# Row stacks by selection matmuls and resident experts in a gated cross-attention and mixture block

## What is computed

```
x  = x + tanh(g0) * attention(layernorm(x), ctx, Wq, Wk, Wv)      # one head of 128, 512 keys per sequence
X  = layernorm(x);  h = rmsnorm(X)
q, k, v = h @ wq, h @ wk, h @ wv                                   # 16 heads of 8
X  = X + softmax(q k^T / sqrt(8)) v @ wo                           # 256 x 256 per head and sequence
h2 = rmsnorm(X);  probs = softmax(h2 @ router)                     # 8 experts, top 2
moe = swiglu(h2, shared) + sum_e combine[:, e] * swiglu(h2, expert e)   # width 256, all 8 experts on all tokens
x  = x + tanh(g1) * (X + moe)
```

## Time and profile before

| | |
|---|---|
| median of 3 runs | 249.63 us |
| the profiled execution's own time | 249.14 us |
| its span, first to last instruction | 247.4 us |
| PE busy | 202.7 us (82%) |
| DVE busy | 152.5 us (62%) |
| ACT busy | 101.3 us (41%) |
| POOL busy | 58.8 us (24%) |
| mean granted TensorE clock | 0.922 |

### The profile page before, as it was taken

The page is one execution under the profiler, slowest core; times in us unless marked ns, Lnnn a source line. Parts: engine busy times, 40 slices in busy tenths (PEclk is TensorE's granted clock), DMA queues, the critical chain, the costliest instruction groups (busy, mean ns, idle before and its releaser), DMA issues.

```text
span 247.4 us, 3838 instructions
## 1 busy us (share of the span) xinstructions
PE 202.7 (82%) x1327; PEld 161.2 (65%) x1327; DVE 152.5 (62%) x393; ACT 101.3 (41%) x203; POOL 58.8 (24%) x77
## 2 busy tenths in 40 slices
PE   7699695659783798299888577899789999999994
PEld 5467464446572566167665455688668888888883
DVE  3779999647653175446687642478874654655653
ACT  8153265930162274246584565423231221221320
POOL 8566969310140020011011011003302332000000
PEclk9999998865679599869999999999979999999999
DMA  6900002535934023400000010000002230000002
GB/s 175 269 0 4 0 16 72 153 104 121 229 103 105 7 90 85 91 3 5 9 1 5 3 48 0 3 0 0 4 0 64 87 107 0 21 3 1 1 3 85
DMA packets 7124, 12.83 MB, mean 52 GB/s; under 512 B 992, under 2 KB 4576, under 8 KB 6592
## 3 DMA queue, kind: packets, MB, share of 16 engines
q1 hardware_dynamic: 7104, 12.58, 19.1%
HBM read 9.69 MB, written 2.62 MB: 50 GB/s over the span
## 4 chain that ended last, share of the span: by engine, by line
PE 48%; DVE 19%; DMA 12%; SPq 11%; issue 3%; ACT 3%; POOL 2%; DVEq 0%; ACTq 0%; POOLq 0%
PE bank L1066 12%; PE bank L1083 7%; PE bank L1085 6%; PE bank L1084 6%; DMA split_scratch<-split 5%; DMA q_st<-negmT 5%; PE bank L1052 5%; SPq L320 4%; SPq L323 4%; PE bank L1037 4%; PE bank L1026 3%; DVE mxs L822 2%; DVE xs L696 1%; DVE small L703 1%; DVE y L690 1%
## 5 line engine op out<-in xcount | busy, mean ns | idle before, releaser
L822 DVE TENSOR_REDUCE mxs<-bank 128x2 f32<-128x512 f32 x64 | 42.5, 689 | 27.9 <-PE bank L1026 27.4
L588 ACT ACTIVATE ep<-bank 128x512 f32<-128x512 f32 x64 | 37.5, 595 | 35.3 <-PE bank L1037 34.7
L1037 PE MATMUL bank<-q_st,k_st 128*128 128x256 f32 x128 | 28.8, 311 | 16.7 <-DMA q_st<-negmT 13.3
L1026 PE MATMUL bank<-k_st,q_st 128*128 128x256 f32 x128 | 34.3, 363 | 2.2 <-DVE mxs L822 1.1
L1066 PEld LDWEIGHTS bank<-down_s,vx 128*128 128x128 f32 x288 | 34.9, 193 | 1.8 <-issue 0.4
L1066 PE MATMUL bank<-down_s,vx 128*128 128x128 f32 x288 | 35.2, 276 | 0.0
L612 ACT ACTIVATE silu<-bank 128x512 f32<-128x512 f32 x28 | 16.6, 598 | 43.9 <-PE bank L1085 43.9
L1037 PEld LDWEIGHTS bank<-q_st,k_st 128*128 128x128 f32 x128 | 21.9, 210 | 18.5 <-DMA q_st<-negmT 13.9
L1083 PE MATMUL bank<-h2hi,whi 128*128 128x512 f32 x72 | 30.8, 428 | 2.7 <-ACT silu L612 2.7
L1026 PEld LDWEIGHTS bank<-k_st,q_st 128*128 128x128 f32 x128 | 23.5, 231 | 10.5 <-issue 4.5
L1085 PE MATMUL bank<-h2hi,wlo 128*128 128x512 f32 x72 | 29.1, 404 | 0.0
(11 more groups left out here) (139 smaller groups left out, 288.4 us busy)
## 6 DMA issues: line engine op xcount, KB each, us to landing
raw<-expert_w SPq DMA_DIRECT2D x9, 256.0 KB, 3.7
split_scratch<-split SPq DMA_DIRECT2D x16, 128.0 KB, 2.2
q_st<-split_scratch SPq DMA_DIRECT2D x16, 128.0 KB
k_st<-split_scratch SPq DMA_DIRECT2D x16, 128.0 KB
down_s<-expert_w SPq DMA_DIRECT2D x9, 128.0 KB, 2.7
ctxT<-ctx_T SPq DMA_DIRECT2D x1, 672.0 KB, 7.7
xs<-x_tiles SPq DMA_DIRECT2D x2, 256.0 KB, 4.2
out_dram<-x SPq DMA_DIRECT2D x2, 256.0 KB, 2.0
```

The costliest lines, as they stand in the source:

```text
L588: nc.scalar.activation(ep[:, n % NEP].rearrange("p t s -> p (t s)"), b_of(("exp", n))[:], ACT.Exp, scale=SCALE_H).then_inc(free(("exp", n) ...
L822: nc.vector.tensor_reduce(mxs[:, n // NH, :, n % NH], b_of(("max", n))[:].rearrange("p (t s) -> p t s", t=TB), AX_X, ALU.max).then_inc(fre ...
L1026: last = pe.matmul(b_of(("max", n))[:, j * L:(j + 1) * L], q_st[:, b % NSTACK, h // 2, j * P:(j + 1) * P], k_st[:, b % NSTACK, k_slot(h), ...
L1037: last = pe.matmul(b_of(("exp", n))[:, j * L:(j + 1) * L], k_st[:, b % NSTACK, k_slot(h), j * P:(j + 1) * P], q_st[:, b % NSTACK, h // 2, ...
```

## The change

Five things change together.

1. **Stacks by matmul.** The DRAM scratch, `stack` and its 12 DMAs per sequence go. Two matrices of zeros and ones (`sel_q` of 96 columns, `sel_k` of 64, per pair of heads; built by POOL from the identity) pick the rows: stage `e` i (four per sequence, 16 in all) does 8 matmuls of 256 columns into two "proj" banks. DVE (sequence 0) or ACT (sequences 1 to 3) copies the q stack, 512 columns, and ACT copies the k stack in two pieces of 512 columns and 32 partitions. There are two stacks instead of three. ACT fills the picking rows twice instead of three times.
2. **Maxima without a DMA.** DVE writes the maxima into columns 64 on of a zeroed tile; the PE transposes 96 columns, and ACT writes the negated rows straight into `q_st`, broadcast to four places (1024 columns), so `place_m` goes.
3. **The order by hand.** The x slots become single steps (`f g xn q s p o n h k w e`) in `FIRST_STEPS`, ahead of the first a slot, and `MIXED_STEPS`, after certain a slots. `LAG` is 12 instead of 13, and the steps after a sequence's last head come one slot earlier.
4. **Experts resident and per sequence.** All nine experts' split weights stay in SBUF. An item is one expert on one sequence: 12 matmuls of 256 columns and half as many down-products; there are 36. Loads no longer wait for places.
5. **Items late.** An item follows every a slot from 76 on. The last exponential of the attention is in slot 63 + 12 = 75, so no item stands ahead of it, `tanh_items` is empty and every item uses Silu. The routing of sequences 2 and 3 falls on slots 90 (first exponential), 92 and 93. The output is stored per sequence.

The core of the diff:

```
-NSTACK = 3
-LAG = 13
+LAG = 12
+NSTACK = 2
-C_STEPS = [("uT0", 31, 31), ("uT1", 32, 32), ("cT", 34, 34), ("wo", 36, 36), ("square", 37, 37), ("h2", 38, 38),
-           ("h2T", 41, 41), ("router", 43, 43)]
-ROUTE_STEPS = [("route_exp1", 43, 43), ("route_top", 45, 45), ("route_exp2", 45, 45), ("route_weights", 46, 46)]
+M_STEPS = [("mT0", 8, 8), ("mT1", 16, 16)]
+C_STEPS = [("uT0", 30, 30), ("uT1", 31, 31), ("cT", 33, 33), ("wo", 35, 35), ("square", 36, 36), ("h2", 37, 37),
+           ("h2T", 40, 40), ("router", 42, 42)]
+ROUTE_STEPS = [("route_exp1", 42, 42), ("route_top", 44, 44), ("route_exp2", 44, 44), ("route_weights", 45, 45)]
+FIRST_STEPS = """f0 g0 xn0 f1 q0 g1 s0 xn1 s1 p0 q1 o0 p1 s2 o1 f2 s3 n0 p2 g2 h0 o2 xn2 p3 k0
+                 e0 q2 e1 o3 e2 w0 e3 n1""".split()
+MIXED_STEPS = {0: "s4 h1", 1: "f3", 2: "k1 s5", 3: "p4 g3", 4: "e4 xn3", 5: "o4 p5", 6: "e5 q3", 7: "o5 s6", 8: "e6 n2",
+               9: "p6 s7", 10: "e7 h2", 11: "o6", 12: "p7 k2", 13: "w1", 14: "o7", 16: "n3", 17: "e8", 19: "h3",
+               21: "e9 k3", 25: "e10", 29: "e11", 31: "w2", 33: "e12", 37: "e13", 41: "e14", 45: "e15", 47: "w3"}
+EARLY_FROM, EARLY_EVERY = 76, 1
...
+            def make_stacks(i):
+                b, part = i // 4, i % 4
...
+                for qk, use, rows in ((0, ("stq", i), sel_q), (1, ("stk", i), sel_k)):
+                    may_fill(pe, use)
+                    for n in range(2):
+                        for hl in range(2):
+                            last = pe.matmul(b_of(use)[0:NSEL if qk == 0 else 64, n * L:(n + 1) * L],
+                                             rows[:, hl, 2 * part + n, :], split[:, b % 2, hl, qk, :],
+                                             start=(hl == 0), stop=(hl == 1))
...
+            def stacks_out(i):
...
+                if b > 0:
+                    is_full(act, ("stq", i))
+                    nc.scalar.copy(q_st[0:NSEL, s, gs:gs + 2, :].rearrange("p g s -> p (g s)"),
+                                   b_of(("stq", i))[0:NSEL]).then_inc(free(("stq", i)), 1)
+                is_full(act, ("stk", i))
                 for p in range(2):
+                    last = nc.scalar.copy(k_st[32 * p:32 * p + 32, s, p * NG + gs:p * NG + gs + 2, :].rearrange("p g s -> p (g s)"),
+                                          b_of(("stk", i))[32 * p:32 * p + 32])
...
-                    nc.scalar.mul(negmT[:, i % 2, :], b_of(use)[0:NH // 2, 0:L], -1.0).then_inc(free(use), 1)
+                    rows = b_of(use)[64:NSEL, 0:L].unsqueeze(1).broadcast_to([32, NG // 2, L])
+                    nc.scalar.mul(q_st[64:NSEL, b % NSTACK, 4 * half:4 * half + 4, :], rows, -1.0).then_inc(free(use), 1)
...
             for stage, i in order:
+                elif stage == "k":
+                    qk_split(i)
+                    if i == 0:
+                        copy_picks(1)
```

More of the change, by code:

```diff
@@ L80, in flamingo_block, with step_of @@
     NHEADS = NB * NH
[L81 to L93, removed]
+    NG = NH // 2
+    NSEL = 96
+    groups = [range(0, 2), range(2, NB)]
+    def step_of(text):
+        return text.rstrip("0123456789"), int(text.lstrip("abcdefghijklmnopqrstuvwxyz"))
     fill_at, read_at = {}, {}
     for b in range(NB):
-        for step, fill, read in M_STEPS + C_STEPS + (ROUTE_STEPS if b % 2 else []):
+        steps = M_STEPS + C_STEPS + (ROUTE_STEPS if b % 2 else [])
+        for step, fill, read in steps:
             fill_at.setdefault(16 * b + fill, []).append((step, b))
@@ new lines, in flamingo_block, with item @@
+    dense = [(0, 0), (0, 1)] + [(e, b) for b in range(2) for e in range(1, NEXP)]
+    dense += [(e, b) for b in range(2, NB) for e in range(NEXP)]
+    ND = len(dense)
+    last_exp = NHEADS - 1 + LAG
+    order = [step_of(text) for text in FIRST_STEPS]
+    begun = 0
+    tanh_items = []
+    def item(n):
+        return [("up", n)] + ([("down", n - 1)] if n else [])
+    for i in range(SLOTS_A):
+        order.append(("a", i))
+        order += [step_of(text) for text in MIXED_STEPS.get(i, "").split()]
+        if i in EARLY_AT or i >= EARLY_FROM and (i - EARLY_FROM) % EARLY_EVERY == 0:
+            order += item(begun)
+            if i <= last_exp:
+                tanh_items.append(begun)
+            begun += 1
@@ new lines, in flamingo_block @@
+    for n in range(begun, ND):
+        order += item(n)
+    order.append(("down", ND - 1))
+    pair_uses = {"turn": [], "proj": [("fold", 0)], "sum": [], "misc": []}
+    for stage, i in order:
+        if stage == "xn":
+            pair_uses["turn"].append(("xnT", i))
+        if stage == "q":
+            pair_uses["proj"] += [("q", i), ("v", i)]
+        if stage == "s":
+            pair_uses["sum"].append(("s", i))
+        if stage == "p":
+            pair_uses["turn"].append(("pT", i))
+        if stage == "o":
+            pair_uses["misc"].append(("o", i))
+        if stage == "h":
+            pair_uses["turn"].append(("hT", i))
+        if stage == "k":
+            pair_uses["proj"].append(("qk2", i))
+        if stage == "w":
+            pair_uses["proj"].append(("v2", i))
+        if stage == "e":
+            pair_uses["proj"] += [("stq", i), ("stk", i)]
@@ L291, in load_expert @@
                          expert_w[e, :, 0:2 * FF]).then_inc(ld_raw[e % NRAW], 16)
[L292 to L332, removed]
+            sp.dma_start(down_s[:, :, e * D:(e + 1) * D],
+                         expert_w[e, :, 2 * FF:3 * FF].rearrange("p (f d) -> p f d", f=2)).then_inc(ld_down[e], 16)
         @block.sync
@@ L862, in _ @@
                 elif stage == "a":
                     a_slot(i)
-                else:
-                    m_third(*thirds[i])
+                elif stage == "up":
+                    dense_up(i)
+                elif stage == "down":
+                    dense_down(i)
         @block.tensor
```

793 lines of the change are left out of this document (378 added, 415 removed).

## The result

The change is slower: 264.41 us in the median (261.8 to 265.73) against 250.25 for the kernel before in the same runs, a ratio of 1.053 (95% interval 1.044 to 1.063). I had forecast 258 us, with 243 to 268 as the range. The profiled execution is the slowest of the four, over 1.5% above the fastest, and the ratio leaves it out. It took 265.73 us over a span of 263.9, so its stretches are compared with my 256.1.

What follows compares the result with a forecast made beforehand. It took PE to bound the kernel, with time to gain only before 111 us, where PE stood still or ran slowly. 161.2 us to the first item plus 94.9 for experts plus 1.74 gave 257.9, said as 258; range 243 to 268.

Steps and rivals of the forecast that it cites:

- Stretch 1: Start to the first slot (first maximum): 44.4 us, bounds 41 to 47, 9 earlier than before.
- Stretch 2: Slots 0 to 11, x work mixed into the first attention: 26 us, bounds 20 to 30.
- Stretch 3: Slots 12 to 16, five exponentials and the start of the pipeline: 7 us, bounds 5.5 to 8.
- Stretch 4: Slots 17 to 48, eight rounds of four slots with a stage e, 5.2 us each: 50.1 us, bounds 41 to 55.
- ACT about 0.85 us idle behind the product: Slots 17 to 48: per round ACT idles about 0.85 us, as the q stack follows the product of four heads.
- ACT is the bound: Slots 17 to 48: ACT, with 4.4 us of work in a 5.2 us round, sets the pace.
- Stretches 5 and 6: Slots 49 to 63, no stage e: 20.5 us; slots 64 to 75, no maxima: 13 us.
- Stretch 7: The experts from slot 76 to the end, 36 items at 2.30 us plus last steps, table loads and tail: 94.9 us.
- the table switches: Slots 90 and 92: four more ACT table loads stall PE 5.5 us, bounds 0 (loads run ahead of waits) to 9.
- (c) No item fills the gaps of the attention's end: End of the attention: named among four causes of the slowdown, no size of its own given.
- The rival of the clock: Stretches 2 to 5: PE granted 1.2 GHz for half of them, 10 us more, so 268 us; chance 0.10.
- The rival of the gaps: Stage e copies ride in ACT's idle gaps, rounds below 4.6 us (above 5 refutes), 238 us; chance 0.20 below 247.1.

Runs made afterwards that it cites:

- the best kernel: Kernel before with maxima written straight into the queries and the twelve early expert thirds moved behind the attention's last products: 230.81 us, ratio 0.924.
- part 2 alone: Kernel before with maxima written straight into the queries, stacks still by DMA: 232.9 us, ratio 0.931.
- the change again: The changed kernel run again with no edit, as base of the comparisons: 265.64 us, ratio 1.064 to the kernel before.
- pads early: Changed kernel with POOL clearing the second stack's pads ahead of the operation that waits for DVE: 258.9 us, ratio 1.035.
- q copies on DVE: Changed kernel with all 16 q stack copies on DVE, none on ACT: 265.53 us, ratio 1.065.
- stacks ahead: Changed kernel with the stack matmuls of slots 17 to 48 one slot earlier, ahead of the product of four heads: 264.92 us, ratio 1.056.
- the run of one table: Changed kernel with tanh-form items until the last routing exponential, two table loads instead of six: 265.04 us, ratio 1.063.
- part 5 alone: Kernel before with its twelve early expert thirds in every slot from 78 on, covering the last steps: 247.83 us, ratio 0.990.
- the copies' width: Changed kernel with ACT copying 8 of each 256 stack columns for sequences 2 and 3: 259.47 us, ratio 1.037.

## Why the prediction was right, and where not

**The sign and the sum** hold, and for the larger part by the named causes; but it is a sum of a large gain and a larger loss, which I never set apart. Luck has a share in it: stretches 1 to 4 came out 13 us longer than forecast and the rest 5 shorter, and the time ended just above the 250 to 264 that I had without the rivals. Set against the best kernel, which has parts 2 and 5, what is left of the change (stacks by matmul, the order by hand, experts per sequence) costs 33.6 us (264.41 less 230.81, from different sessions; by the ratios 1.053 and 0.924 it is 32). By the two sets of windows, 17.1 us of the span's difference of 36.5 lie before the first product (87.40 against 70.35), 21.5 in the 60 slots (84.90 against 63.45), and the experts gain 2.0. Part 2 gave 17 us back. My own list had both in one and never priced part 2 alone; its rows, two DMA pieces of 6.40 and 6.51 us in the chain, would have given 13 for the waits.

**Stretch 1** (first maximum): 44.4 forecast with bounds 41 to 47, 47.59 and 44.84 measured. Right within the 3 us by which the two executions differ.

**Stretch 2**: 26 forecast with bounds 20 to 30, 31.0 measured, and 33.0 in the change again. The step that failed is one I didn't have: POOL's queue. I walked PE, ACT and DVE through the list and left the clearing of the second stack's pads at nothing. It was worth 6.7 us (pads early), 5.5 of them in this stretch, which then took 27.5: the largest gain by moving one call.

**Stretch 3**: 7 forecast, 8.8 measured. It isn't the clock, which was 1.00 there. PE waited 1.8 us for DVE's maxima before it could transpose the first half (L942), a wait that my sum lacks.

**Stretch 4**: 50.1 forecast, 53.3 measured; a round 5.2 against 5.5. The size held, the reason in part only. "ACT about 0.85 us idle behind the product" falls: with the stacks ahead of the product no time came back. "ACT is the bound" falls too: over 87.4 to 140.7 us ACT was busy 40.53 of 53.30 us and PE 47.14. With the copies all but gone a round is still 4.8, since the new matmuls fill PE. What bounds it is both engines taking turns over two banks, a theory that fits the failures of the two runs that eased ACT (q copies on DVE, stacks ahead), but that no run with more banks has shown.

**Stretches 5 and 6**: 33.5 forecast, 30.1 measured to the first item (140.68 to 170.76). The last three rounds, which have no maxima, took 3.4 to 3.6 us, with 3.4 forecast; what was too big lies in the steps and routing added on top, and no run took those apart.

**Stretch 7**: 94.9 forecast, 93.1 measured. The term that was too big is that of the table switches, 5.5 us; an item was 2.31 us (227.35 to 229.66), as forecast. The timeline of ACT in the kernel after:

```profile
204.32 1.28 ACT L537 ACT_TABLE_LOAD   x1
206.60 0.23 ACT L537 ACTIVATE rt<-rt 128x32 f32<-128x32 f32 x1 [0.99 <-DVE rt L710]
206.85 1.28 ACT L568 ACT_TABLE_LOAD   x1
...
209.38 1.28 ACT L540 ACT_TABLE_LOAD   x1
213.78 0.21 ACT L540 ACTIVATE rs<-rs 128x4 f32<-128x4 f32 x1 [3.11 <-DVE rs L723]
214.00 1.28 ACT L568 ACT_TABLE_LOAD   x1
```

The loads for the exponential start at 204.32 and 209.38, before DVE's result is there: they run ahead of the wait, as my lower bound had it, and only the loads back to Silu are in the way. PE's waits in this part were 2.6 us, all for DVE. The Trainium skill ("ScalarE: Activation LUTs", section "What ACT_TABLE_LOAD costs") puts a switch at some 2.66 us with a drain: none is seen here, Silu begins 1.29 us after the load's start at 206.85. The same page of the Trainium skill, section "Table sets: the hidden batching unit", advises batching by set; done here, in the run of one table, it gave nothing: DVE was late instead. Two slips of addition stand in the prediction: with 5.5 us more for the drains its sum is 263.4, not 263.8, and its stretches 1 to 6 add up to 161.0, not 161.2.

**"(c) No item fills the gaps of the attention's end"** was named as a loss and is none. With items from slot 62 the change is as slow, and part 5 alone makes the kernel before 1% faster. In this kernel an item put beside the exponentials delays them.

**The rival of the clock** had a real mechanism at another place. In the rounds the clock was 0.94; it fell before the first exponential:

```profile
26.00:50.00 24.00, 17.58 (x80) 14.48 (x78) 11.11 (x29) 10.75 (x15) 3.80 (x5) 0.67 0.00 1
```

In the change again it was 0.86 there and 0.76 from 50 to 78 us. As a loss against the kernel before it doesn't count: the mean clock is 0.935, against 0.922.

**The rival of the gaps** fails at its own mark: rounds above 5 us.

Open: how the 33.6 us part between the selection matmuls and the order by hand. Clearing the pads early takes 6.7 and the copies' width 6.2 of them; whether these two add up wasn't run, nor the stacks by matmul alone in the kernel before. The selection matmuls are 23.6 us of PE's recorded busy time, part of it beside other matmuls.

## What to carry to other kernels

When a change removes waits of two kinds, price each alone by its own row. Here PE waited 13.3 us for the small DMAs of the maxima, and replacing them alone gave 16.9 us. For the large DMAs of the stacks PE waited 0.9 us, though their trip also stands in the chain ahead of the first slot; replacing them put 44 copies on ACT and 128 matmuls on PE, the two engines that are busiest in the attention's 60 slots (47.6 and 54.5 of 63.5 us in the best kernel). Walk every queue through the new order, POOL's among them: one clearing behind one wait cost 6.7 us. Before filling an engine's gaps, ask who waits for its next result: here the exponentials did, and the items gained nothing.

## What the runs showed of the hardware

ACT's copy out of PSUM took the same time for 32 partitions as for 96 (575 and 581 ns at 512 columns). Groups of the kernel after (mean ns behind the busy time):

```profile
L501 ACT CAST k_st<-bank 32x512 fp32r<-32x512 f32 x32 | 18.4, 575 | 4.4 <-PE bank L930 4.0
...
L497 ACT CAST q_st<-bank 96x512 fp32r<-96x512 f32 x12 | 7.0, 581 | 10.3 <-PE bank L930 5.6 <-POOL k_st L355 4.4
```

The k stack, taken in two pieces of 32 partitions, thus costs about twice what one piece would, an estimate: no run copied it in one piece. And a pair of DVE's operations between SBUF tiles took longer beside POOL's memset. The timeline of the kernel with part 2 alone has the same pair of operations free and beside one:

```profile
6.75 0.60 DVE L640 TENSOR_SCALAR y<-xs,mv,small 128x128 f32<-128x128 f32 x2 [0.90 <-POOL small L378]
...
10.00 1.98 DVE L640 TENSOR_SCALAR y<-xs,mv,small 128x128 f32<-128x128 f32 x2 [0.23 <-POOL small L378]
10.02 1.80 POOL L394 MEMSET q_st<- 64x2048 f32 x1
```

0.60 us against 1.98. I had priced the norm's operations beside a clearing at 1.85 from a row of that kind; what I had not looked at is how cheap they are without it, by a factor of three. No run moved the clearings out of their way. The Trainium skill ("SBUF — State Buffer", section "SBUF: two separate sides") says that VectorE in its faster two-port modes and GpSimd hold a common pair of ports each for a whole instruction, while the other stands. Whether these operations run in such a mode no row shows; the rows agree in that the pair of operations ends 0.16 us after the memset it met (11.98 against 11.82). The memset took 1.80 us, as the ones at 58.22 and 60.07 above did.
